# A one-core tower kernel: four places for routed results instead of two, the first weights loaded in two halves, and five small moves

## What is computed

```python
h = gelu(codebook[x] @ W1 + b1) @ W2 + b2                 # 256 -> 1024 -> 256
h = h + mingru(layernorm(h))                              # 2 layers, a scan along each of the 2 sequences
n = layernorm(h)
shared = (gelu(n @ w1s) * (n @ w2s)) @ w3s                # 256 -> 1024 -> 256, for every token
idx = argmax(n @ Wg)                                      # one of 8 experts for each token
routed = (gelu(n @ W1[idx]) * (n @ W2[idx])) @ W3[idx]    # only the token's own expert
out = h + shared + routed
```

## Time and profile before

| | us |
|---|---|
| median of 3 executions (lowest, highest) | 489.27 (489.18, 489.71) |
| the profiled execution, its own time | 489.65 |
| its span, first to last instruction | 487.9 |
| PE busy | 477.8 |
| DVE busy | 330.0 |
| ACT busy | 247.0 |
| POOL busy | 82.7 |

### The profile page before, as it was taken

How to read it: one execution, slowest core, us unless ns; L and a number is a source line. 1 busy time by engine, 2 the same in 40 slices (tenths; PEclk the granted TensorE clock), 3 DMA queues, 4 the chain that set the end, 5 groups by cost and what they waited for, 6 DMA issues and landing times.

```text
span 487.9 us, 8515 instructions
## 1 busy us (share of the span) xinstructions
PE 477.8 (98%) x3052; PEld 427.0 (88%) x3053; DVE 330.0 (68%) x540; ACT 247.0 (51%) x376; POOL 82.7 (17%) x92
## 2 busy tenths in 40 slices
PE   8999999999999999999999999999999999999995
PEld 7898888888888887888788999799999998999885
DVE  3559678578686868868645587646785776777463
ACT  3767774575653463443334556336545473555321
POOL 5431031011011001102460002100200021020351
PEclk9999999999999999999999999999999999999999
DMA  5942121001210002200444455505553356250372
GB/s 156 378 129 85 34 75 55 32 23 48 66 62 1 1 0 93 83 0 23 151 145 79 171 171 201 194 24 182 187 196 145 134 199 215 97 194 14 113 270 93
DMA packets 25543, 55.12 MB, mean 113 GB/s; under 512 B 7264, under 2 KB 18784, under 8 KB 21536
## 3 DMA queue, kind: packets, MB, share of 16 engines
q1 hardware_dynamic: 19472, 43.58, 26.5%
q0 software_dynamic: 2976, 8.14, 4.9%
q10 hardware_dynamic: 3056, 2.88, 2.0%
HBM read 42.25 MB, written 12.35 MB: 112 GB/s over the span
## 4 chain that ended last, share of the span: by engine, by line
PE 81%; DVE 10%; ACT 3%; issue 3%; DMA 1%; POOL 1%; another core or an unknown queue 1%; DVEq 0%; POOLq 0%
PE ps L278 22%; PE ps L279 21%; PE ps L280 21%; PE ps L791 6%; PE ps L793 3%; PE ps L821 2%; DVE hT L1213 1%; DVE w_slots L1241 1%; DVE ps L1219 1%; DVE stats L1278 1%; DMA q<-codebook_in,idx_sb 1%; PE ps L605 1%; PE ps L823 1%; PE ps L640 1%; ACT hT L966 1%
## 5 line engine op out<-in xcount | busy, mean ns | idle before, releaser
L278 PE MATMUL ps<-xW,w_slots 128*128 128x256 f32 x256 | 73.6, 287 | 0.1
L280 PE MATMUL ps<-xW,w_slots 128*128 128x256 f32 x256 | 72.4, 283 | 0.0
L279 PE MATMUL ps<-xW,w_slots 128*128 128x256 f32 x256 | 72.4, 283 | 0.0
L1213 DVE TENSOR_TENSOR hT<-ps,hT 128x512 fp32r<-128x512 f32 x64 | 43.9, 686 | 36.6 <-ACT hT L955 17.1
L476 POOL DMA_INDIRECT y_tokens<-y_rows,row_ids x30 | 36.1, 1203 | 188.1 <-DVE y_rows L1595 169.6
L1575 DVE TENSOR_TENSOR w_slots<-stage,w_slots 128x2048 fp32r<-128x2048 f32 x24 | 54.8, 2285 | 3.3 <-ACT w_slots L1103 2.7
L278 PEld LDWEIGHTS ps<-xW,w_slots 128*128 128x128 f32 x256 | 48.7, 190 | 0.9 <-DVE xW L1347 0.3
L279 PEld LDWEIGHTS ps<-xW,w_slots 128*128 128x128 f32 x256 | 48.8, 191 | 0.0
L280 PEld LDWEIGHTS ps<-xW,w_slots 128*128 128x128 f32 x256 | 48.7, 190 | 0.0
L966 ACT ACTIVATE hT<-ps 128x512 fp32r<-128x512 f32 x32 | 19.1, 597 | 54.6 <-DVE ps L1219 53.0
L791 PE MATMUL ps<-w_slots,hW 128*128 128x512 f32 x128 | 46.6, 401 | 0.0
(11 more groups left out here) (208 smaller groups left out, 1277.1 us busy)
## 6 DMA issues: line engine op xcount, KB each, us to landing
stage<-ew_in SPq DMA_DIRECT2D x24, 1024.0 KB, 4.8
x_sorted<-zero_row SPq DMA_DIRECT2D x16, 128.5 KB
x_sorted<-zero_odd SPq DMA_DIRECT2D x16, 128.5 KB
stage<-w1s_in SPq DMA_DIRECT2D x2, 1024.0 KB, 7.8
fetched<-y_tokens SPq DMA_DIRECT2D x4, 512.0 KB, 5.6
x_pair<-x_sorted ACTq DMA_DIRECT2D x7, 256.0 KB, 2.8
out_rows<-fetched SPq DMA_DIRECT2D x3, 512.0 KB, 3.0
first_stage<-tok_w_in SPq DMA_DIRECT2D x1, 1024.0 KB
```

Source lines behind the costliest of these rows:

```text
L278: pe.matmul(dst, lhs_hi, rhs_hi, start=start, stop=False, skip_group_check=shares_bank)
L279: pe.matmul(dst, lhs_hi, rhs_lo, start=False, stop=False, skip_group_check=shares_bank)
L280: return pe.matmul(dst, lhs_lo, rhs_hi, start=False, stop=stop, skip_group_check=shares_bank)
L1213: dve.tensor_tensor(hT[:, c % RING, 1, :], ps[:, bank, :], f32(hT[:, c % RING, 0, :]), ALU.subtract).then_inc(h_lo, 1)
```

## The change

It has these parts. Chunk numbers are those of the tables.

1. `tok_w1` is loaded in two halves of 512 KB. The first goes out where the whole did; the second when the first two gathers have landed, ahead of `tok_w2`'s quarters, which still wait for the third. ACT and DVE split the second half of `w1p` later: ACT behind `first_q_hi`, DVE behind `q_lo(0)`.
2. Piece 3 of the shared weights is split after chunk 11 instead of 9.
3. Unit 7's product (line 1312) is put off by a chunk, to just ahead of its scan (`late_product`).
4. The statistics for the second norm of block 2 move from behind chunk 38's units to chunk 36, ahead of unit 13; the copy of block 1's logits moves up, to between the two halves of `unit_value(15)`.
5. `y_rows` has four places (`WAYS = 4`) and `y_tokens` four spare tiles; the scatter loop lets three stores be under way. `y_rows` and `xTp` change regions.
6. Zero rows all come from one `zero_row`. Ids are floats; two new operations of DVE on 128 x 30 (`spread_unread`, in expert 0) turn them into integers and spread the rows without a token over the four spare tiles. GpSimd's scatter loop waits for them.
7. Of the last block's four output tiles the second and fourth are stored from ACT's queue.

```diff
-    SPLIT_PIECES = {7: (0,), 8: (1, 2), 9: (3,), 11: (4,), 12: (5,), ...
+    SPLIT_PIECES = {7: (0,), 8: (1, 2), 11: (3, 4), 12: (5,), ...
...
-            sp.dma_start(first_stage[:, 0, :], tok_w1.rearrange("p k n -> p (k n)")).then_inc(w1_land, 16)
+            w1v = first_stage[:, 0, :].rearrange("p (k n) -> p k n", k=KD)
+            sp.dma_start(w1v[:, :, 0:NB], tok_w1[:, :, 0:NB]).then_inc(w1_land[0], 16)
...
-            for i in range(BT - 1):
+            for i in range(2):
                 sp.wait_ge(first_land[i], 16)
+            sp.dma_start(w1v[:, :, NB:HID], tok_w1[:, :, NB:HID]).then_inc(w1_land[1], 16)
+            sp.wait_ge(first_land[2], 16)
...
-            sp.wait_ge(y_stored[0], ((back + 1) >> 1) * 16)
-            sp.wait_ge(y_stored[1], (back >> 1) * 16)
+            for p in range(WAYS):
+                sp.wait_ge(y_stored[p], ((back + (WAYS - 1 - p)) >> 2) * 16)
...
-            for i in range(BT):
+            for i in range(0, BT, 2):
                 t = (BLOCKS - 1) * BT + i
                 sp.wait_ge(summed, BLOCKS + i)
                 sp.dma_start(out_v[:, t, :], fetched[:, t, :]).then_inc(out_stored, 16)
...
+            pool.iota(unread_by[:], [[0, 2 * WAYS], [P, WAYS]], base=0, channel_multiplier=0,
+                      allow_small_or_imprecise_dtypes=True).then_inc(pool_const, 1)
...
-            pool.wait_ge(ids_land, 16)
+            pool.wait_ge(ids_done, 1)
             for i in range(XT):
                 pool.wait_ge(y_taken, i + 2)
                 to_tokens(i)
-                if i:
-                    pool.wait_ge(y_stored[(i - 1) % 2], 16 * ((i - 1) // 2 + 1))
+                if i >= WAYS - 1:
+                    j = i - (WAYS - 1)
+                    pool.wait_ge(y_stored[j % WAYS], 16 * (j // WAYS + 1))
                     pool.sem_inc(y_free, 1)
...
-            act.wait_ge(w1_land, 16)
-            for h in range(2):
+            def w1_hi_half(h):
                 cols = slice(h * NB, (h + 1) * NB)
+                act.wait_ge(w1_land[h], 16)
                 act.activation(w1p[:, 0, :, cols], w1v[:, :, cols], ACT.Copy).then_inc(w1_hi, 1)
...
+            w1_hi_half(0)
             first_q_hi()
+            w1_hi_half(1)
             q_hi(0)
...
+            for i in range(1, BT, 2):
+                t = (BLOCKS - 1) * BT + i
+                act.wait_ge(summed, BLOCKS + i)
+                act.dma_start(out_v[:, t, :], fetched[:, t, :]).then_inc(out_stored, 16)
...
             w1_lo_half(0)
             first_q_lo()
+            q_lo(0)
             w1_lo_half(1)
-            q_lo(0)
...
+            late_product = {25}
...
                 if c - 1 in late_scan and c < MLP:
+                    if c - 1 in late_product:
+                        unit_product(late_scan[c - 1])
                     unit_scan(late_scan[c - 1])
...
                 for u in UNIT.get(c, ()):
+                    if u == UNITS - KD - 1:
+                        row_stats(2, 2)
+                        row_moments(2, 2)
                     unit_value(u)
+                    if u == UNITS - 1:
+                        copy_logits(LOG_END[c])
+                    if c not in late_product:
+                        unit_product(u)
                     if c not in late_scan:
                         unit_scan(u)
...
+            def spread_unread():
+                dve.wait_ge(ids_land, 16)
+                dve.scalar_tensor_tensor(out=unread[:], in0=row_ids[:], scalar=float(TILES * P), in1=unread_by[:, 0:XT],
+                                         op0=ALU.is_ge, op1=ALU.mult).then_inc(unread_done, 1)
+                dve.wait_ge(unread_done, 1)
+                dve.tensor_tensor(to_rows[:], row_ids[:], unread[:], ALU.add).then_inc(ids_done, 1)
...
                 if opening:
                     add_rows(BLOCKS - 2)
                     single_rows_lo(0)
+                    spread_unread()
```

More of the change, by code:

```diff
@@ L164, in build @@
         x_pair = at("x_pair", [P, 2, D], F32, r_xl)
[L165 removed]
+        y_rows = at("y_rows", [P, WAYS * D], F32, r_ring + 24 * K)
         hW = at("hW", [P, PAIRS, 2, NB], F32R, r_ring)
         xW = at("xW", [P, 2, 2, KD, WINDOW], F32R, r_ring + 16 * K)
[L169 removed]
+        xTp = at("xTp", [P, 2, KD, P], F32R, r_xl + 2 * K)
         xb_first = at("xb_first", [P, 2, KD, NB], F32R, r_xb)
@@ L217, in build @@
         turns = small("turns", [P, TOTAL + 1], U16)
-        r_one = place[0]
-        zero_odd = small("zero_odd", [P, D + 1])
-        x_one = at("x_one", [P, D], F32, r_one)
+        x_one = small("x_one", [P, D])
         singles = small("singles", [P, EXPERTS])
@@ L226, in build @@
         row_ids = small("row_ids", [P, XT])
+        unread = small("unread", [P, XT])
+        unread_by = small("unread_by", [P, 2 * WAYS * WAYS])
+        to_rows = small("to_rows", [P, XT], I32)
         ps = ctx.enter_context(nc.psum_tensor("ps", [P, 8, NB], F32))
@@ L244, in build @@
         idx_land = sem("idx_land"); small_land = sem("small_land"); b2_land = sem("b2_land"); share_land = [sem(f"share_land{c}") for c in range(3)]
-        w1_land = sem("w1_land"); w2_land = [sem(f"w2_land{n}") for n in range(4)]; gru_land = sem("gru_land")
+        w1_land = [sem(f"w1_land{h}") for h in range(2)]; w2_land = [sem(f"w2_land{n}") for n in range(4)]; gru_land = sem("gru_land")
         expert_land = [sem(f"expert_land{c}") for c in range(3)]; early_land = [sem(f"early_land{c}") for c in range(3)]
@@ L268, in build @@
         gT_ps = sem("gT_ps"); gT_hi = sem("gT_hi"); gT_lo = sem("gT_lo")
-        tile_done = sem("tile_done"); y_taken = sem("y_taken"); y_stored = [sem(f"y_stored{p}") for p in range(2)]; y_free = sem("y_free")
+        tile_done = sem("tile_done"); y_taken = sem("y_taken"); y_stored = [sem(f"y_stored{p}") for p in range(WAYS)]; y_free = sem("y_free")
         fetch_land = [sem(f"fetch_land{b}") for b in range(BLOCKS)]
@@ L476, in to_tokens @@
                 pool.indirect_dma_start(
-                    out=y_tokens, out_offset=bass.IndirectOffsetOnAxis(ap=row_ids[:, i:i + 1].bitcast(I32), axis=0),
-                    in_=y_rows[:, i % 2 * D:(i % 2 + 1) * D], in_offset=None,
-                    bounds_check=(TILES + 2) * P - 1, oob_is_err=True).then_inc(y_stored[i % 2], 16)
-            pool.wait_ge(ids_land, 16)
+                    out=y_tokens, out_offset=bass.IndirectOffsetOnAxis(ap=to_rows[:, i:i + 1], axis=0),
+                    in_=y_rows[:, i % WAYS * D:(i % WAYS + 1) * D], in_offset=None,
+                    bounds_check=(TILES + WAYS) * P - 1, oob_is_err=True).then_inc(y_stored[i % WAYS], 16)
+            pool.wait_ge(ids_done, 1)
             for i in range(XT):
@@ L485, in _ @@
                 to_tokens(i)
-                if i:
-                    pool.wait_ge(y_stored[(i - 1) % 2], 16 * ((i - 1) // 2 + 1))
+                if i >= WAYS - 1:
+                    j = i - (WAYS - 1)
+                    pool.wait_ge(y_stored[j % WAYS], 16 * (j // WAYS + 1))
                     pool.sem_inc(y_free, 1)
-            pool.wait_ge(y_stored[(XT - 1) % 2], 16 * ((XT - 1) // 2 + 1))
+            for j in range(XT - (WAYS - 1), XT):
+                pool.wait_ge(y_stored[j % WAYS], 16 * (j // WAYS + 1))
         @block.tensor
@@ L1180, in _ @@
                 shared_hi(c)
+            out_v = out.rearrange("(t p) d -> p t d", p=P)
+            for i in range(1, BT, 2):
+                t = (BLOCKS - 1) * BT + i
+                act.wait_ge(summed, BLOCKS + i)
+                act.dma_start(out_v[:, t, :], fetched[:, t, :]).then_inc(out_stored, 16)
         @block.vector
```

38 lines of the change are left out of this document (17 added, 21 removed).

## The result

| | before | changed |
|---|---|---|
| median beside each other on one chip, six executions each | 489.43 | 485.26 |
| lowest to highest | 489.18 to 489.71 | 484.15 to 485.97 |
| ratio, 95% interval | | 0.9914 [0.9899, 0.9928] |
| the profiled execution, its own time | 489.65 | 485.6 |
| its span | 487.9 | 483.8 |

The change gains 4.2 (3.5 to 4.9 by the interval), where 2.6 were forecast; 485.26 lies 0.3 under the low end of the range. The last two rows tell where to look: 1.84 of the gain comes ahead of the last matmul, where 2.2 were forecast, and 2.29 behind it, where 0.35 were.

What follows compares the result with a forecast made beforehand. TensorE's work, busy 98% of the span, was taken as the bound, with about 10 us idle. Terms 0.3 + 0.46 + 0.33 + 1.15 + 0.35 = 2.59 (2.6) gave 487.05 against 489.65, or 486.7 from the median; range 485.6 to 488.2.

Steps and rivals of the forecast that it cites:

- The sign: Whole kernel: the change makes it faster, chance 0.89; same 0.08, slower 0.03.
- the five places of TensorE: TensorE's late starts at 12.95, 45.59, 113.01, 190.33 and 192.69, which the change touches; they sum to 2.36.
- Start: Loading W1 in halves: fourth gather lands 0.2 to 0.6 earlier, cutting TensorE's 0.42 wait at tile 3; 0.3 taken.
- rival A: Start gives it back: second half or `tok_w2`'s first quarter comes late, ScalarE waits; costs 0.3 to 1.6; chance 0.16.
- The 3.2 for the load of 512 KB: W1's second half, by 2.0 fixed plus bytes at 436 GB/s: lands 3.2 after issue, at 10.8, hidden.
- Piece 3: x1 transposes of block 0: without the piece ahead of the statistics, TensorE's wait of 0.46 goes; gain 0.46.
- Unit 7's product: Accumulator of block 3: with the product no longer ahead of `take_rows`, TensorE's wait of 0.33 goes; gain 0.33.
- Logits and statistics: Logits' turn and state's transposes near 190 and 192: TensorE's waits of 0.39 and 0.76 go; gain 1.15.
- rival B: New wait replaces a removed one, likely in chunk 36 or chunk 11: 487.2 to 487.6; chance 0.10.
- Four places: Routed stage, `y_rows`: VectorE waited 2.0 for a place, TensorE never, and GpSimd's ten scatters had slack; gain 0.
- Rival C: Routed stage gains after all, VectorE's 2.0 of waits reaching TensorE: 484.7; chance 0.04.
- Tail: Last stores: last one issued from ScalarE's queue at 483.43 instead of SyncE's at 483.78; gain 0.35.

Runs made afterwards that it cites:

- W1 whole and the ids late: Changed kernel with W1 in one load (part 1 undone) and VectorE's two id operations moved behind the window's lo half of expert 0: 484.54, ratio 0.9888.
- before again: The kernel before the change, unaltered, profiled a second time: 488.97, ratio 0.9976.
- GpSimd late: Changed kernel, four places kept, with GpSimd's program made to wait for VectorE's last sum before it ends: 488.7, ratio 0.9982.
- all stores from SyncE: Changed kernel with part 7 undone, all four last stores issued from SyncE's queue: 486.12, ratio 0.9919.

## Why the prediction was wrong

The sign and the five places of TensorE were right. The size was not, since the largest single gain had been put at nothing. By its steps:

- **Start, 0.3 forecast: 0.04 in the profile, and about -0.6 on the mean.** The second half landed at 11.9 to 12.8 in seven profiles, and in four of them behind the 12.26 by which it had to be there (half of 2.00 is 1.00 and not 1.05, but the rounding measured 1.06). The fourth gather's issue became shorter, but the third was not stretched in its place (1.02, as before 1.01), and the fourth landed no earlier on the mean: the step from its issue to its landing failed. So did the sentence that `tok_w2`'s quarters behind it "compete with the fourth gather as before". I followed the fourth gather and the second half, and only named the first quarter in rival A: it is due at once behind tiles 2 and 3, and came 1.09 late. Rival A, at 0.16, was right about the start. And 0.42 of one execution stood for a wait that a second execution does not have. The 3.2 for the load of 512 KB, worked out in the prediction by a rule of the Trainium skill, is not borne out: it took 4.1 to 5.0. That rule was fitted to DMAs that GpSimd issues, and this one is SyncE's.
- **Piece 3, 0.46: 0.52. Unit 7's product, 0.33: 0.41.** Right, by the profiles; the difference is the refill of the pipeline, which I had put into the range and not into the sum. The work that was moved found idle time in both cases, and no new wait of TensorE came of it. The times of the runs are too coarse to show either term.
- **Logits and statistics, 1.15: 1.24** by the profile, 0.84 between medians. Right. Chunk 36 took the 1.6 of statistics without a wait, so rival B did not come.
- **Four places, 0: 1.9. This is the step that failed.** I checked whether TensorE or VectorE waited for a place, found that TensorE did not the earlier trace rows, and put GpSimd's ten late scatters at nothing, since the fetches had slack. The question left out was when GpSimd's own program ends. Its last scatter goes out at 479.99, TensorE's last matmul ends at 482.93, and the drain of 5.137 starts in between, at 482.55. Rival C (the routed stage gains, 484.7) gave nearly the right time by the wrong mechanism: VectorE's 2.0 of waits for a place are unchanged.
- **Tail, 0.35: 0.40** where the scatters are early. The chain of stores was sized rightly and was not the end of the program: SyncE was done at 485.8 and the span was 487.9. With two places the 0.35 alone would have shortened nothing, as in the run with two places, where GpSimd's drain ends 2.1 after SyncE's. The two numbers stood side by side in the trace and I did not subtract them.
- **Not forecast: the wait in expert 0**, which by chance took 0.4 back in the execution compared.

With 1.9 for part 5, nothing for the start and the other terms as forecast (0.46, 0.33, 1.15, 0.35) the sum is 4.2, which is the gain that was measured. That it fits to a tenth is partly luck. By what the two profiled executions show, the terms are 0.04 + 0.52 + 0.41 + 1.24 + 1.9 + 0.40, less 0.42 for the waits that come and go: 4.1, and these two executions are 4.05 apart.

## What to carry to other kernels

Before pricing a tail, name the queue whose last instruction ends the span, its drain included, and subtract: an engine that has long been idle for the work can still set the end. In this kernel that engine was GpSimd, whose work has to end more than 5.1 us ahead of the last output. A load that is moved ahead of others in a queue can make those others late: follow the next one to the engine that needs it. Compare at least two profiles of the same kernel before counting a wait under half a microsecond at the start, or one that the profile puts down to "issue".

## What the runs showed of the hardware

GpSimd's closing drain took 5137 ns in all 14 profiles, whether it began 1.6 after the issue of the last scatter had ended (482.55 after 480.96, before) or, with GpSimd held back, 11 after it (481.38 after 470.48). Why it takes that long no run shows.

GpSimd's issue of a gather is held by VectorE's split of `w1p` (two inputs in SBUF) only if the split is already running when the issue begins. In the changed kernel the split begins in the middle of the third gather's issue and leaves it at its usual length, and the fourth begins while the split runs:

```profile
6.62 1.23 DVE L1215 TENSOR_TENSOR w1p<-first_stage,w1p 128x1024 fp32r<-128x1024 f32 x1 [5.21 <-ACT w1p L944]
6.21 1.02 POOL L424 DMA_INDIRECT q<-codebook_in,idx_sb  x1 [0.30 <-issue]
7.53 1.21 POOL L424 DMA_INDIRECT q<-codebook_in,idx_sb  x1 [0.30 <-issue]
```

In the 12 profiles in which the fourth begins during a split it ends 0.88 to 0.90 behind that split and takes 1.01 to 2.00. In the 11 cases in which a split begins during an issue, the issue takes 1.01 or 1.02. So the stretch of 0.92 in before was a matter of when the split began, and would be gone with W1 whole too if it began 0.2 later: with W1 whole and the ids late it did (7.65, against the gather's 7.62), and the issue took 1.01.

The waits in expert 0 seem to follow the instruction queue. The trace of the transfers has packets of 16 KB on a queue of the kind "instruction" (number 8); for which engine they are it does not say. In the changed kernel one ends at 269.10, TensorE had come to the place at 269.1, and it went on at 270.70. In all 12 profiles with a wait there, it goes on 1.50 to 1.67 behind the end of such a packet (before again: 270.41 to 271.93; GpSimd late: 268.64 to 270.24). Packets of 8 KB on a second such queue end nearby too, at distances that differ by more than a microsecond. In the two without, before (270.80) and all stores from SyncE (267.73), TensorE came to it 1.7 behind the packet and did not wait. Runtime: NRT & Kernel Launch (Instruction fetch mechanics) of the Trainium skill says that instructions are fetched in blocks of 16 KB and that a branch to a block that is not there waits for it; this part of the program stands behind branches. The rows fit that. It is argued from the records and not tested, and what lets the packet come earlier in some executions stays open.
